# Linear-attention layers: the MLP's second layer and its LayerNorm one pass later, with a third PSUM bank and separate MLP weights

## The reference, cut to what matters

```
for i in range(8):
    residual = x
    Q  = elu(x @ Wq[i] + bq[i]) + 1          # 16 heads x 64
    Kf = elu(x @ Wk[i] + bk[i]) + 1
    V  = x @ Wv[i] + bv[i]
    KV, sumK = sum(Kf * V, over tokens), sum(Kf, over tokens)
    att = Q * KV / (Q * sumK + 1e-6)
    y = gelu(att @ Wo[i] + bo[i])
    x = layer_norm(y + residual) * ln1_s[i] + ln1_b[i]
    residual = x
    h = gelu(x @ W1[i] + b1[i])              # 128 -> 512
    h = gelu(h @ W2[i] + b2[i])              # 512 -> 128
    x = layer_norm(h + residual) * ln2_s[i] + ln2_b[i]
```

## Time and profile before

| | us |
|---|---|
| median of 3 runs | 6107.69 |
| lowest and highest | 6101.62, 6109.22 |
| the profiled execution's own time | 6111.76 |
| its span, first to last instruction | 6109.9 |
| mean granted TensorE clock in it | 0.889 |

### The profile page before, as it was taken

How to read it: one execution, slowest core, us unless ns; L and a number is a source line. 1 busy time by engine, 2 the same in 40 slices (tenths; PEclk the granted TensorE clock), 3 DMA queues, 4 the chain that set the end, 5 groups by cost and what they waited for, 6 DMA issues and landing times.

```text
span 6109.9 us, 74475 instructions
## 1 busy us (share of the span) xinstructions
PE 4812.9 (79%) x19786; PEld 2830.8 (46%) x19786; DVE 3789.8 (62%) x11610; ACT 2987.0 (49%) x5250; POOL 1120.0 (18%) x1540
## 2 busy tenths in 40 slices
PE   4788888858888888888888888888588447788864
PEld 2677777743333333333333333333255335555543
DVE  4455544567777767667767767767656744444466
ACT  1100000017888778787877878778122124444421
POOL 1000000022222222222222222222200012222210
PEclk9888888879999999999999999999799768899976
DMA  1000000000000000000000000000000001111100
GB/s 45 1 1 1 1 1 1 1 18 1 1 18 1 14 4 6 13 1 18 0 14 4 0 18 0 14 4 0 0 0 0 0 26 43 42 47 48 45 3 14
DMA packets 103971, 71.55 MB, mean 12 GB/s; under 512 B 59092, under 2 KB 97705, under 8 KB 100025
## 3 DMA queue, kind: packets, MB, share of 16 engines
q1 hardware_dynamic: 103608, 67.64, 3.8%
HBM read 55.89 MB, written 11.73 MB: 11 GB/s over the span
## 4 chain that ended last, share of the span: by engine, by line
PE 44%; DVE 24%; issue 13%; ACT 8%; DMA 6%; POOL 2%; SPq 1%; DVEq 1%; ACTq 0%; POOLq 0%
PE bank L1489 7%; DMA packed_dram<-arena 4%; PE bank L1522 4%; PE bank L1503 4%; PE bank L1211 3%; DVE arena L1653 3%; PE bank L1516 3%; DVE arena L1639 3%; PE bank L1208 3%; DVE arena L1622 2%; DMA arena<-packed_dram 2%; PE bank L1200 2%; DVE arena L1278 2%; DVE arena L1664 2%; DVE arena L1630 1%
## 5 line engine op out<-in xcount | busy, mean ns | idle before, releaser
L1489 PE MATMUL bank<-arena 128*128 (+1 forms) x3072 | 1471.8, 616 | 13.7 <-ACT arena L1551 12.1
L1489 PEld LDWEIGHTS bank<-arena 128*128 128x128 f32 x3072 | 598.1, 199 | 742.4 <-issue 709.5
L1622 DVE SCALAR_TENSOR_TENSOR arena<-arena 128x256 f32<-128x256 f32 x1024 | 391.9, 421 | 776.6 <-ACT arena L1551 772.4
L1503 PE MATMUL bank<-arena 128*128 128x512 f32 x1024 | 564.6, 634 | 219.8 <-DVE arena L1653 218.6
L1564 ACT ACTIVATE arena<-arena,const_table 128x256 f32<-128x256 f32 x1024 | 558.5, 600 | 79.0 <-POOL arena L1691 78.9
L1691 POOL TENSOR_SCALAR arena<-arena 128x512 f32<-128x512 f32 x512 | 316.7, 618 | 1354.5 <-DVE arena L1633 1347.1
L1639 DVE SCALAR_TENSOR_TENSOR arena<-bank,bv,arena 128x256 f32<-128x256 f32 x1024 | 450.4, 478 | 0.0
L1653 DVE SCALAR_TENSOR_TENSOR arena<-arena 128x256 f32<-128x256 f32 x1024 | 448.8, 480 | 0.7 <-issue 0.7
L1550 ACT ACTIVATE arena<-bank,bqk 128x512 f32<-128x512 f32 x512 | 350.0, 684 | 160.3 <-PE bank L1489 133.8
L1503 PEld LDWEIGHTS bank<-arena 128*128 128x128 f32 x1024 | 167.9, 191 | 556.6 <-DVE arena L1653 503.0
L1633 DVE SCALAR_TENSOR_TENSOR arena<-bank,bqk,arena 128x512 f32<-128x512 f32 x512 | 384.4, 751 | 18.1
(11 more groups left out here) (338 smaller groups left out, 8845.0 us busy)
## 6 DMA issues: line engine op xcount, KB each, us to landing
arena<-packed_dram SPq DMA_DIRECT2D x96, 192.0 KB
packed_dram<-arena SPq DMA_DIRECT2D x48, 192.0 KB, 8.4
arena<-packed_dram SPq DMA_DIRECT2D x16, 576.0 KB
arena<-in_L_attn_Wk_dram SPq DMA_DIRECT2D x16, 256.0 KB, 3.1
arena<-in_L_attn_Wq_dram SPq DMA_DIRECT2D x16, 256.0 KB, 3.8
arena<-in_L_attn_Wv_dram SPq DMA_DIRECT2D x16, 256.0 KB, 4.1
arena<-in_L_attn_Wo_dram SPq DMA_DIRECT2D x8, 512.0 KB, 3.8
arena<-in_L_attn_W_dram SPq DMA_DIRECT2D x16, 256.0 KB, 3.0
```

What stands on the lines that cost most here:

```text
L1489: nc.tensor.matmul(bank[:, RING1[m % 5], :], w1p[k][:, i * P:(i + 1) * P], zT_of(g), start=True, stop=True).then_inc(a1_proj.sem, 1)
L1503: nc.tensor.matmul(bank[:, 6, :], wo1[:, i, :], a1_att[:, i % 4, :], start=(i == 0), stop=(i == NB1 - 1)).then_inc(a1_outd.sem, 1)
L1622: last = nc.vector.scalar_tensor_tensor(seqs(a1_kf[:, i % 2, :])[q], seqs(a1_ek[:, i % 2, :])[q], 1.0, seqs(a1_kf[:, i % 2, :])[q], ALU.mi ...
```

## The change

The second layer of the MLP, its activation, residual and LayerNorm run one pass later than the first layer, with lag 3 in place of 2. In the lists:

- TensorE: `mlp_pe` is parted into `h_pe` (lag 2, w = 2) and `h2_pe` (lag 3, w = 1). The first layer uses banks 0, 1, 6 and 0 (`HBANK`), the second layer bank 1. `h_pe` waits before block 1 for the second layer's activation, before block 2 for y's, before block 3 for block 0's.
- ScalarE: in the Gelu block `h2_act` (lag 3) comes first, then `y_act`, then the four of `h_act`.
- GpSimd: `residual_pool(1)` (lag 3) ahead of `residual_pool(0)`; the root of the second LayerNorm keeps its place at w = 4.
- VectorE: statistics of the second LayerNorm at w = 4 in place of 3, its application at w = 6 in place of 5. Its way back on TensorE and ScalarE is at w = 7 in place of 6.
- `a1_x1` is doubled; `a1_fin` shares memory with `a1_h`. W1 and W2 have a semaphore each, and each is reloaded after its own last use; so with the biases, which makes four hooks. `over_layers` writes four passes out and loops over four, and runs three passes after the last layer in place of two.

```diff
--- before.py
+++ after.py
@@ -140,22 +140,23 @@
     def one_layer(layer, low):
         parts = parts_of(layer)
         opening()
-        for s in range(2):
+        for s in range(4):
+            if s == 2:
+                opening()
             hooks[s](layer)
             slot(parts, s, low, G)
-        hooks[2](layer)
-        with eng.Fori(0, (G - 2) // 2) as j:
+        with eng.Fori(0, (G - 4) // 2) as j:
             opening()
             for v in range(2):
                 for lag, fn in parts:
-                    fn(2 * j + (2 + v - lag), (v - lag) % 2)
+                    fn(2 * j + (4 + v - lag), (v - lag) % 2)
 
     one_layer(0, 0)
     with eng.Fori(1, layers) as layer:
         one_layer(layer, -G)
     parts = parts_of(layers - 1)
     opening()
-    for s in range(G, G + 2):
+    for s in range(G, G + 3):
         slot(parts, s, 0, G)
 
 
@@ -1386,16 +1387,17 @@
-            a1_x1 = scratch("a1_x1", [P, GT])
+            a1_x1 = scratch("a1_x1", [P, 2, GT])
-            a1_fin = scratch("a1_fin", [P, 2, GT])
+            a1_fin = a1_h[:, 0:2, :]
...
@@ -1458,10 +1461,12 @@
                         a1_outd.wait(sp, layer * G - 1)
                     sp.dma_start(wo1[:], one("Wo").rearrange("l (b p) d -> p (l b) d", p=P)).then_inc(a1_wo_loaded, 16)
                     if not first:
+                        a1_h_psum.wait(sp, layer * G - 1)
+                    sp.dma_start(w1a[:], one("W1").rearrange("l d f -> d (l f)")).then_inc(a1_w1_loaded, 16)
+                    if not first:
                         a1_h2_psum.wait(sp, layer * G - 1)
-                    sp.dma_start(w1a[:], one("W1").rearrange("l d f -> d (l f)")).then_inc(a1_mlp_loaded, 16)
                     sp.dma_start(w1b[:], one("W2").rearrange("l (b p) d -> p (l b) d", p=P))\
-                        .then_inc(a1_mlp_loaded, 16)
+                        .then_inc(a1_w2_loaded, 16)
 
                 if n:
                     x_written.wait(sp, n * G - 1)
@@ -1499,33 +1504,55 @@
 
 
                             a1_y_act.wait(nc.tensor, t - 1)
-                            a1_h2_act.wait(nc.tensor, t - 2)
+                            if not before_all(g, 2):
+                                a1_h_act.wait(nc.tensor, t - 2, 3)
                         nc.tensor.matmul(bank[:, 6, :], wo1[:, i, :], a1_att[:, i % 4, :],
                                          start=(i == 0), stop=(i == NB1 - 1)).then_inc(a1_outd.sem, 1)
                     return fn
 
-                def mlp_pe(g, u):
+                def weights_of(g):
+                    return layer if isinstance(g, int) and g < 0 else layer + 1
+
+                def before_all(g, back):
+
+                    return isinstance(layer, int) and layer == 0 and isinstance(g, int) and g < back
+
+                def h_pe(g, u):
                     t = turn(g)
-                    before = isinstance(g, int) and g < 0
-                    nc.tensor.wait_ge(a1_mlp_loaded, 32 * (layer if before else layer + 1))
+                    nc.tensor.wait_ge(a1_w1_loaded, 16 * weights_of(g))
                     a1_x1d.wait(nc.tensor, t)
+                    for i in range(NF1):
+                        if i == 1:
+                            a1_h2_act.wait(nc.tensor, t - 1)
+                        if i == 2:
+                            if isinstance(g, int) and g == G - 1:
+                                a1_y_act.wait(nc.tensor, t)
+                            else:
+                                a1_y_act.wait(nc.tensor, t + 1)
+                        if i == 3:
+                            a1_h_act.wait(nc.tensor, t, 1)
+                        nc.tensor.matmul(bank[:, HBANK[i], :], w1a[:, i * P:(i + 1) * P], a1_x1[:, u, :],
+                                         start=True, stop=True).then_inc(a1_h_psum.sem, 1)
+
+                def h2_pe(g, u):
+                    t = turn(g)
+                    nc.tensor.wait_ge(a1_w2_loaded, 16 * weights_of(g))
+                    a1_h_act.wait(nc.tensor, t)
                     a1_zt.wait(nc.tensor, t - 1)
                     for i in range(NF1):
-                        if i >= 2:
-                            a1_h_act.wait(nc.tensor, t, i - 1)
-                        nc.tensor.matmul(bank[:, i % 2, :], w1a[:, i * P:(i + 1) * P], a1_x1[:],
-                                         start=True, stop=True).then_inc(a1_h_psum.sem, 1)
-
-                    a1_y_act.wait(nc.tensor, t if isinstance(g, int) and g == G - 1 else t + 1)
-                    for i in range(NF1):
-                        a1_h_act.wait(nc.tensor, t, i + 1)
-                        last = nc.tensor.matmul(bank[:, 6, :], w1b[:, i, :], a1_h[:, i, :],
+                        last = nc.tensor.matmul(bank[:, 1, :], w1b[:, i, :], a1_h[:, i, :],
                                                 start=(i == 0), stop=(i == NF1 - 1))
                     last.then_inc(a1_h2_psum.sem, 1)
 
                 def turn_in_pe(i):
                     def fn(g, u):
-                        lns[i]["in"].wait(nc.tensor, turn(g))
+                        t = turn(g)
+                        lns[i]["in"].wait(nc.tensor, t)
+
+                        if i == 0 and not before_all(g, 1):
+                            a1_h_act.wait(nc.tensor, t - 1)
+                        if i == 1 and not (isinstance(g, int) and g == G - 1):
+                            a1_h_act.wait(nc.tensor, t + 1, 2)
                         for q in range(QT):
                             last = nc.tensor.transpose(bank[:, i, q * P:(q + 1) * P], a1_r[:, i, q * P:(q + 1) * P],
                                                        ident)
@@ -1586,11 +1613,14 @@
                         a1_h_psum.wait(nc.scalar, t, i + 1)
                         if i == 0:
                             a1_h2_psum.wait_free(nc.scalar, t)
-                        nc.scalar.activation(a1_h[:, i, :], bank[:, i % 2, :], ACT.Gelu_apprx_tanh,
+                        nc.scalar.activation(a1_h[:, i, :], bank[:, HBANK[i], :], ACT.Gelu_apprx_tanh,
                                              bias=b11[:, i:i + 1]).then_inc(a1_h_act.sem, 1)
+
+                def h2_act(g, u):
+                    t = turn(g)
                     a1_h2_psum.wait(nc.scalar, t)
-                    lns[1]["in"].wait_free(nc.scalar, t)
-                    nc.scalar.activation(a1_g2[:], bank[:, 6, :], ACT.Gelu_apprx_tanh, bias=bd1[:, 3:4])\
+                    lns[1]["in"].wait(nc.scalar, t - 1)
+                    nc.scalar.activation(a1_g2[:], bank[:, 1, :], ACT.Gelu_apprx_tanh, bias=bd1[:, 3:4])\
                         .then_inc(a1_h2_act.sem, 1)
 
                 def exp_table_act(g, u):
@@ -1603,7 +1633,7 @@
                         if i == 0:
 
                             lns[1]["in"].wait_free(nc.scalar, t)
-                            nc.scalar.activation(a1_x1[:], bank[:, 0, :], ACT.Identity, bias=bd1[:, 2:3],
+                            nc.scalar.activation(a1_x1[:, u, :], bank[:, 0, :], ACT.Identity, bias=bd1[:, 2:3],
                                                  scale=bd1[:, 1:2]).then_inc(a1_x1d.sem, 1)
                         else:
                             apart(nc.scalar)
...
@@ -1730,23 +1760,30 @@
                     dve.append((0, feature_dve(w)))
                     of(dve, att_dve, w - 2)
                     of(pool, query_pool, w - 1)
+                    if w == 1:
+                        pe.append((3, h2_pe))
                     if w == 2:
-                        pe.append((2, mlp_pe))
-                        act += [(1, gelu_table_act), (1, y_act), (2, h_act), (1, exp_table_act)]
-                        pool += [(1, residual_pool(0)), (2, residual_pool(1))]
+                        pe.append((2, h_pe))
+                        act += [(1, gelu_table_act), (3, h2_act), (1, y_act), (2, h_act), (1, exp_table_act)]
+                        pool += [(3, residual_pool(1)), (1, residual_pool(0))]
                     if w == 3:
-                        pe += [(1, turn_in_pe(0)), (2, turn_in_pe(1))]
-                        dve += [(1, norm_stats_dve(0)), (2, norm_stats_dve(1))]
+                        pe += [(1, turn_in_pe(0)), (3, turn_in_pe(1))]
+                        dve.append((1, norm_stats_dve(0)))
                     if w == 4:
-                        pool += [(1, norm_rstd_pool(0)), (2, norm_rstd_pool(1))]
+                        pool += [(1, norm_rstd_pool(0)), (3, norm_rstd_pool(1))]
+                        dve.append((3, norm_stats_dve(1)))
                     if w == 5:
-                        dve += [(1, norm_dve(0)), (2, norm_dve(1))]
+                        dve.append((1, norm_dve(0)))
                     if w == 6:
-                        pe += [(1, turn_back_pe(0)), (2, turn_back_pe(1))]
-                        act += [(1, back_act(0)), (2, back_act(1))]
+                        dve.append((3, norm_dve(1)))
+                        pe.append((1, turn_back_pe(0)))
```

(25 more changed lines are left out.)

5 lines of the change are left out of this document (3 added, 2 removed).

## The result

The changed kernel takes 6129.14 us (median of 7 runs, 6123.70 to 6153.28) against 6100.29 of the kernel before (7 runs, 6096.46 to 6109.22): a ratio of 1.0052, 95% interval 1.0036 to 1.0068. It is slower, as forecast, but by 29 us, not by 73. The profiled execution took 6124.16 us, its span is 6121.9, 12.0 more than the span before; it is one of the fastest of the seven.

The account below looks back on a forecast made before the run. The prediction took no single engine as the bound but a loop of waits among VectorE, ScalarE and TensorE. Terms 6 + 54 + 13 = +73 us on the profiled 6111.8 us gave 6181 us against the median, range 6060 to 6260.

Parts of the forecast that it names:

- The sign and the path: Whole kernel: slower, chance 0.68, with the moved second layer's matmuls at w1 delaying ScalarE's exponential of w2.
- the clock: TensorE's new 2.2 us wait in the Gelu block: 36 of 64 blocks run slow at 1.5 us each, +54 us.
- the edges: Layer boundaries: fourth bias hook and earlier table load at the third pass, +3 us; low clock after layer changes, +5.
- The end: Extra pass after the last layer, running one chain of second layer and norm alone: +5 us, bounds -3 and +12.
- The lag costs its matmuls at w1: TensorE's queue at w1: eight second-layer matmul instructions delay everything behind them by 3.44 us per pass.
- the rival that the second layer hides: TensorE at w1: the 3.44 us cost nothing, 220 us come off, 5961 us; hidden wholly or in part, chance 0.18.
- The Gelu block falls to 6.92 us: ScalarE's block from Gelu table load to first exponential: shrinks by 4.84 us in A passes (opening table load), 3.15 in others.
- The norms: Second LayerNorm's later statistics delay the w5 query step; VectorE waits 0.5 us at w6, 1.0 us per pair.
- A pair at full clock: Two consecutive passes of the linear-attention stage, without clock falls: +0.2 us, +6 over 32 pairs.
- the upper half: Clock term's range 0 to +154 us: its higher part was called likelier, by the skill page on PSUM bank cycling.
- the fourth hook as a loss: Fourth pass of each layer: a bias hook makes ScalarE wait for VectorE, as at the second pass (1.68 us).
- The +5 for a lower clock at w1 and w2 behind a layer change: After each layer change: eight more matmuls run at low clock there, 0.8 us more, +5 us.

Follow-up runs that it names:

- e9: Changed kernel with only one of the second layer's four products and block 0's first-layer product made three times (output not the reference's): 5942.81 us, ratio 0.9732.
- e5: Changed kernel with the second LayerNorm's statistics, application and way back returned to w3, w5 and w6, lag 3 kept: 6143.26 us, ratio 1.0061.
- e6: Changed kernel with block 0's product made three times, second-layer products ahead of w1's output product, second LayerNorm back at w3, w5, w6: 6008.91 us, ratio 0.9834.
- e10: Changed kernel with block 0's product made three times and second-layer products ahead of w1's output product, LayerNorms as changed: 6021.06 us, ratio 0.9857.
- e12: Changed kernel with second-layer products at w2 before the first layer, y's activation first, second LayerNorm back at w3, w5, w6: 5948.25 us, ratio 0.9746.
- e11: Changed kernel with second-layer products moved from w1 to w2, between output product and first layer, y's activation first: 5964.51 us, ratio 0.9769.
- e2: Changed kernel with the second layer's products at w1 put ahead of the output product: 6057.41 us, ratio 0.9927.
- e4: Changed kernel with only one of the second layer's four products, so output is not the reference's: 6011.89 us, ratio 0.9849.
- e1: Changed kernel with block 0's first-layer product made three times to fill TensorE's wait in the Gelu block: 6104.18 us, ratio 1.0001.
- e3: Kernel before with the third bank alone (first layer in banks 0, 1, 6, 0; lag 2 kept): 6022.28 us, ratio 0.9868.
- e7: Kernel before with only the new over_layers: four passes written out, empty fourth hook, third pass's table load ahead of its hook: 6099.42 us, ratio 0.9979.

## Why the prediction was right in its sign and wrong in its size

The sign and the path were right. Two terms of the sum failed: the clock, +54 forecast and 23 measured, and the edges, +8 forecast and -22 measured. The end was forecast too small, which hid a part of it. One by one:

- *The lag costs its matmuls at w1.* Right. Forecast 3.44 us per pass behind the wait for VectorE; ScalarE's new waits are 3.54 in A and 3.38 in B (3.5 to 4 forecast), and e9 prices three quarters of the products at 2.57 us per pass. So the rival that the second layer hides is out, though weight loads are busy in only 36% of the stage (1030.88 of 2877.00). The section that the prediction cites for it (the Trainium skill, Perfetto Trace Analysis, Identifying the Most-Contended Engine) names the share of peak FLOP/s beside the share of weight loads; the prediction used the second alone.
- *The Gelu block falls to 6.92 us.* Right: 6.91.
- *The norms.* Right in the mechanism: query step waited for 4.20 us (about 4 forecast), VectorE idle at w6 for 0.43 (0.5 forecast). What this costs hangs on the blocks: e5 undoes it on the changed kernel and gains nothing, with seven more slow blocks; e6 against e10 and e12 against e11 undo it where no block is slow and gain 14 and 16 us. TensorE's wait at w5 falls from 2.3 to 1.0 us (1.2 forecast).
- *A pair at full clock: +0.2 us.* It is -0.2: 88.47 against 88.64, -5 us over 32 pairs in place of +6. This lies between the 88.8 us that was to show the sum right and the 88 that was to show it wrong.
- *The clock term: this step failed.* The wait was foreseen to 0.02 us (2.2; it is 2.22), and what a slow block costs nearly so (1.5; it is 1.7). But "I take it that somewhat over half of the new blocks run slow (36 of 64)" made a frequency out of a length. The wait is 2.21 or 2.22 us in all full blocks but one (2.14), and 16 are slow. With the same wait 28 are slow in e2, 45 in e4 and 23 in e5; with 0.50 us none is, in e1. The term was +54 us; e1 prices it at 23 (2876.7 - 2853.7). What decides which of the equal waits is followed by a fall is not shown. What the Trainium skill (TensorE: Matmul & The Clock Gate, section A second HAM failure mode: psum-queue depth-cycling) says of short idle times, and I took to favour the upper half, is borne out in kind (the clock does swing behind such waits) and not in amount. The cycle through three banks alone does not bring it about: e3 cycles through the same three, with waits of 0.98 to 1.65 us, and has no slow block.
- *The edges: +8 us, the second step that failed.* With its 23 us for the clock taken off, the changed stage is 2853.7 us, 27.5 less than before. Pairs account for 5; the other 22 are at the layers' edges. There I had priced the fourth hook as a loss and the table load ahead of the third hook as 1.3 us. The second is nearly right: 1.5 us in e7, some 12 us over the eight layers. The +5 for a lower clock at w1 and w2 behind a layer change did not come: the wait at w2 there is 5.24 us and was 1.91, 3.3 more and not 3.44 + 0.8. Block to block, the kernel before against e1, the third pass of a layer falls from 47.6 to 45.3 us, the fourth grows from 44.6 to 45.3, and the first falls from 50.1 to 49.4 (means; the first numbers hold blocks in which the clock fell). What brings the remaining 10 of the 22 us is open.
- *The end: +5 us, with a bound of +12.* It is +14.4. From the last projections of TensorE to the first final transpose (L1760 before, L1797 after) before, then after:

```profile
4267.19 2.74 PE L1489 MATMUL bank<-arena 128*128 x6
...
4299.71 3.60 PE L1522 MATMUL bank<-arena 128*128 128x512 f32 x8
...
4313.61 0.69 PE L1760 MATMUL bank<-const_table,arena 128*128 128x128 f32 x2 [2.00 <-POOL arena L1754]
```

```profile
4260.64 2.74 PE L1494 MATMUL bank<-arena 128*128 x6
...
4289.54 5.16 PE L1543 MATMUL bank<-arena 128*128 128x512 f32 x8 [1.04 <-ACT arena L1640]
...
4305.32 5.80 PE L1543 MATMUL bank<-arena 128*128 128x512 f32 x8 [1.04 <-ACT arena L1640]
...
4321.42 1.97 PE L1797 MATMUL bank<-const_table,arena 128*128 128x128 f32 x8 [2.00 <-POOL arena L1791]
```

From 4267.19 to 4313.61 are 46.4 us before, from 4260.64 to 4321.42 60.8 after: the extra pass runs one more second layer and norm with nothing beside them.

Of the span's 12.0 us the stage gives -4.5, its end +14.4, the stages behind +4.2 and the start -2.1. This accounts for the two profiled executions, which are 12.4 us apart, and not for the 29 us between the medians: the profiled execution before took 11.5 us more than the 6100.29, the one after 5.0 less than the 6129.14. Why the timed runs of the changed kernel lie up to 29 us above its profiled one is not shown directly; that their spread falls from 30 to 7 us when the wait is filled speaks for the number of slow blocks.

## What to carry to other kernels

Work moved to a later pass to shorten one engine's stall has to be put into a queue somewhere: look at what stands behind it there, and put it where that engine itself waits (here a few list entries further on, ratio 1.0052 against 0.9769) and not ahead of what the stalled engine wants next. Try each part of a change alone: here one more bank was worth 1.3%, and the whole change lost it. And count the falls of TensorE's clock on both sides before judging an edit: taking out the same products brought 117 us where 29 blocks more became slow, and 161 where none did.

## What was not expected of the hardware

- Waits of equal length (2.21 to 2.22 us) are followed by the lower clock level in one block and not in the next. In the blocks before the change, 25 of 28 waits of 1.93 or 1.94 us were followed by it and none of 22 of 1.84 or 1.85; in e7 5 of 6 of 1.86 us were. The same wait 0.50 us long never was.
- A fall of the clock does not cost the same everywhere. A slow block costs 1.7 us. In e12 the clock falls 33 times, each time behind a wait of 2.3 us or more ahead of an output product, in e11 4 times, and e12 is still 16 us faster.
- Work for nothing can pay: making block 0's product three times (four more matmul instructions, 1.7 us) took 25 us off the kernel and three quarters off its spread.
